# A decoder layer on one core: the same instructions, stepped through in another order on each of five engines

## The reference

```
x = x + attn(layernorm(x))            # stage a: 8 heads of 128, one shared key and value head, causal mask
x = x + xattn(layernorm(x), ctx, ...) # stage b: 16 heads of 16 over a context of 256,
                                      #   with a bias per batch, head, row and column, and a key mask
x = x + moe(layernorm(x))             # stage c: gate picks 2 of 8 experts, and one shared FFN;
                                      #   hidden = square(relu(x @ w1)), out = hidden @ w2
```

## Time and profile before

| | |
|---|---|
| median of 3 runs | 2403.15 us (2397.21 to 2403.51) |
| the profiled execution, its own time | 2400.63 us |
| its span | 2398.8 us |
| granted TensorE clock, mean over the span | 0.954 of full speed |
| busy: TensorE, VectorE, ScalarE, GpSimd | 2130.8, 1987.0, 2079.4, 1786.7 us |
| DMA traffic | 367.16 MB, 153 GB/s on average |

### The profile page before, as it was taken

One profiled execution on the slowest core, in us unless ns is written; L12 is line 12 of the kernel. 1 busy time (PEld: TensorE's weight loads), 2 busy tenths in 40 slices (PEclk: granted clock), 3 DMA queues, 4 the chain that ended last, 5 costly groups with the idle time before them and its releaser, 6 DMA issues.

```text
span 2398.8 us, 73036 instructions
## 1 busy us (share of the span) xinstructions
PE 2130.8 (89%) x24128; PEld 1855.2 (77%) x24128; DVE 1987.0 (83%) x6672; ACT 2079.4 (87%) x6065; POOL 1786.7 (74%) x1899
## 2 busy tenths in 40 slices
...
GB/s 148 113 173 155 168 146 162 171 153 160 159 155 142 173 157 158 162 155 138 169 155 164 161 157 163 145 174 160 161 163 156 150 147 158 162 160 157 142 145 22
DMA packets 711784, 367.16 MB, mean 153 GB/s; under 512 B 561392, under 2 KB 659952, under 8 KB 711408
## 3 DMA queue, kind: packets, MB, share of 16 engines
...
## 4 chain that ended last, share of the span: by engine, by line
PE 48%; DVE 21%; issue 14%; ACT 13%; POOL 2%; DMA 2%; SPq 0%; DVEq 0%; ACTq 0%; POOLq 0%
PE ps_a_misc L965 13%; PE ps_c_hidden L965 10%; PE ps_c_out L965 9%; PE ps_a_scores L1025 4%; DVE b_neg_scores L828 3%; DVE g_mask L898 2%; PE ps_b_misc L1102 2%; PE ps_b_scores L1088 2%; ACT ps_b_probs L664 2%; PE ps_a_misc L1044 2%; DVE b_probs_hi_lo L835 2%; ACT ps_b_probs L662 2%; ACT b_probs_hi_lo L672 2%; DVE g_weights L920 1%; DVE g_sum L913 1%
## 5 line engine op out<-in xcount | busy, mean ns | idle before, releaser
L520 POOL TENSOR_TENSOR bias<-bias,b_mask 128x512 f32<-128x512 f32 x512 | 646.4, 1274 | 7.2 <-DMA bias<-in_bias 7.0
L835 DVE TENSOR_TENSOR b_probs_hi_lo<-ps_b_probs,b_probs_hi_lo 128x512 f16<-128x512 f32 x512 | 351.8, 687 | 128.9 <-ACT b_probs_hi_lo L672 127.3
L828 DVE CUSTOM_DVE_ANT_0 b_neg_scores<-ps_b_scores,bias 128x256 f32<-128x256 f32 x1024 | 389.3, 417 | 72.0 <-PE ps_b_scores L1088 60.4
L534 POOL TENSOR_TENSOR c_hidden<-c_relu 128x512 f32<-128x512 f32 x288 | 299.8, 1041 | 152.7 <-ACT c_relu L690 138.0
L541 POOL TENSOR_TENSOR c_hidden_lo<-c_hidden,c_hidden_hi 128x512 f16<-128x512 f32 x288 | 334.2, 1160 | 59.8 <-issue 39.4
L662 ACT ACTIVATE ps_b_probs<-b_neg_scores,b_neg_max 128x256 f32<-128x256 f32 x512 | 245.4, 479 | 144.0 <-DVE b_probs_hi_lo L835 108.7
L965 PE MATMUL ps_c_hidden<-c_xT_hi,w_hi 128*128 128x256 f16 x1152 | 325.1, 282 | 40.1 <-ACT c_relu L690 40.0
L965 PE MATMUL ps_c_out<-w_hi,c_hidden_hi 128*128 128x256 f16 x1152 | 316.1, 274 | 29.0 <-DVE acc L936 28.9
L965 PE MATMUL ps_c_hidden<-c_xT_lo,w_hi 128*128 128x256 f16 x1152 | 324.0, 281 | 0.0
L965 PE MATMUL ps_c_hidden<-c_xT_hi,w_lo 128*128 128x256 f16 x1152 | 323.6, 281 | 0.0
L965 PE MATMUL ps_c_out<-w_hi,c_hidden_lo 128*128 128x256 f16 x1152 | 316.3, 275 | 0.0
...
## 6 DMA issues: line engine op xcount, KB each, us to landing
bias<-in_bias SPq DMA_DIRECT2D x256, 512.0 KB, 4.1
q_stack<-qk_scratch SPq DMA_DIRECT2D x256, 64.0 KB, 3.6
...
k_stack_even<-qk_scratch SPq DMA_DIRECT2D x128, 64.0 KB, 2.9
```

The lines of the kernel that those rows point to most:

```text
L520: gp.tensor_tensor(part, part, b_mask[:, :], ALU.add).then_inc(b_c_ok, 1)
L534: gp.tensor_tensor(c_h[:, :], c_r[:, e % 2, :], c_r[:, e % 2, :], ALU.mult).then_inc(c_sq_ok, 1)
L828: last = dve.tensor_tensor_reduce(out=b_t[:, u, c, :], in0=ps_bs[:, c * T:(c + 1) * T], in1=bias[:, slot, at:at + T], scale=-2.0, scalar=3 ...
L835: dve.tensor_tensor(b_p2[:, j % DEPTH, :, 1, :], ps_bp[:, :].rearrange("p (c t) -> p c t", c=CT), b_p2[:, j % DEPTH, :, 0, :], ALU.subtrac ...
```

## The change

The table ORDERS is replaced by another one. Each engine's list holds the same entries as before, 33 for SP, 47 for GpSimd, 111 for ScalarE, 120 for VectorE, 89 for TensorE; their order, their lags and the place where a list begins differ. No step's code is touched. The file grows by a line, so that each line of code behind the table has a number higher by one in the changed kernel. The diff, cut to the first and last rows of TensorE's list:

```
@@ -74,48 +74,49 @@
...
     tensor="""
-        a_s:5@3 c_f2:8@6 a_s:6@3 b_wo:0@5 a_pt:2@3 a_pv:1@3 a_s:7@3 b_s:0@4 b_s:1@4 a_pt:3@3 a_pv:2@3 c_T:0@5
...
-        c_f2:7@5 b_pv:13@4 b_pv:14@4 b_pv:15@4 a_s:4@2 a_pt:1@2 a_pv:0@2 b_o:0@4""",
+        b_pv:1@4 c_f2:1@5 c_f1:5@5 b_s:7@4 a_pt:6@3 b_pv:2@4 a_pv:5@3 c_f2:2@5 b_s:8@4 c_f1:6@5 a_pt:7@3
...
+        b_s:0@3 a_s:7@2 b_s:1@3 c_T:0@4 a_pt:4@2 b_s:2@3 c_gate:0@4 c_f1:0@4 b_s:3@3 a_pv:3@2 c_f1:1@4 b_s:4@3
+        c_f1:2@4 a_pt:5@2 c_f2:0@4 b_s:5@3 c_f1:3@4 a_pv:4@2 b_pv:0@3 b_s:6@3 c_f1:4@4""",
```

More of the change, by code:

```diff
@@ L76 @@
     sync="""
[L77 to L80, removed]
+        b_pT:8@5 b_pT:9@5 b_pT:10@5 b_load:5@5 b_pT:11@5 b_pT:12@5 b_split_q:0@4 a_T:0@3 b_pT:13@5 b_load:6@5
@@ L81 @@
+        b_store_q:0@4 b_load:7@5 b_pT:14@5 b_store_k:0@4 b_pT:15@5 b_stack_q:0@4 b_stack_k:0@4 b_load:0@4
+        c_f2:8@6 b_pT:0@4 b_mask:0@4 b_pT:1@4 b_load:1@4 a_ln:0@3 b_pT:2@4 b_pT:3@4 b_load:2@4 b_pT:4@4 b_pT:5@4
+        b_load:3@4 b_pT:6@4 b_pT:7@4 b_load:4@4""",
     gpsimd="""
-        b_comb:9@5 b_comb:10@5 b_comb:11@5 c_lo:4@6 c_f1:5@6 c_lo:5@6 c_f1:6@6 b_comb:12@5 a_ln:0@3 b_ln:0@4
-        b_comb:13@5 b_comb:14@5 a_kv:0@3 b_comb:15@5 c_lo:6@6 a_q:0@3 b_split_q:0@4 c_f1:7@6 c_lo:7@6
```

64 lines of the change are left out of this document (33 added, 31 removed).

## The result

The changed kernel takes **2438.43 us** (median of 4 runs, 2437.49 to 2439.81) against 2400.52 us for the kernel before (4 runs, 2397.21 to 2403.51): a ratio of 1.0159, 95% interval 1.0141 to 1.0177. It is slower by 38 us; the prediction said 10 us faster, with a range that ended at 2434. Lines of code have numbers higher by one.

A forecast was written before the change was run, and what follows sets the result against it. The prediction took no single engine as the bound, only holes between steps: 2400.6 - 13 (31 periods at 70.05 instead of 70.46 us) + 3.5 (filling) = 2391, stated as 2390 us, range 2352 to 2434.

The forecast's parts named there:

- The stall of q and k: TensorE's wait before b_s:0 for copies filling q_stack and k_stacks; predicted gone with its slow clock, 47 us less.
- The payback: New waits the change brings in each period: 0.5 to 2.5 us, taken at 1.1.
- Stage a later: a_kv and a_q:0 move behind b_s:15 on TensorE; claimed to cost nothing by itself.
- a_v_lo: VectorE's a_kv, ahead of b_s:15, waits for its input from TensorE: 0 to 1.4 us per period, taken at 0.3.
- c_f1:8 behind c_f2:4: ScalarE's relu waits for this later FFN product on TensorE: 0.5 to 1.1 us per period, taken at 0.8.
- GpSimd, priced at nothing: GpSimd's b_split_k ahead of a_kv and context split ahead of a_q:3; claimed free, otherwise a_s:6 late by one piece.
- Filling: Time before the first a_wo: last four weight pieces come after a_pv:7 of batch 0, +3.5 us (0 to +6).
- Draining: Stage c of the last batch keeps its order: 0, give or take 3 us.
- A reordering leaves every busy number as it is: All engines: claimed that reordering changes no busy time and can move only the holes between steps.
- Rival 2: End of stage a holds b_s:0 every period, TensorE waiting for VectorE (a_oT_lo), clock 0.95: 2430 us, chance 0.27.
- Rival 3: No change: the holes only move, held by stage a's chain or c_f1:8's relu: 2400 to 2404 us, chance 0.15.
- the rule beside it: Improve the most-contended engine; taken strictly, a change that takes nothing off any engine would leave 2400 us.

The follow-up runs named there:

- e9: Kernel before, order untouched, with six of the eight copies of the k stack left out (low-order products of stage b's scores missing): 2360.75 us, ratio 0.9838.
- e8: Kernel before with one part of the change alone, stage b's transpose and query projection ahead of stage a's: 2451.79 us, ratio 1.0199.
- e3: Changed kernel with a_kv on VectorE moved behind b_s:15 and b_p:14: 2462.97 us, ratio 1.0265.
- e7: Kernel before with c_f2:4 behind a_wo and c_f1:8 behind b_s:12 on TensorE, and matching moves on VectorE and ScalarE: 2422.83 us, ratio 1.0084.
- e6: Changed kernel with c_f1:8 put ahead of c_f2:4 on TensorE, directly behind a_wo: 2461.48 us, ratio 1.0248.
- e5: Changed kernel with b_pv:3, b_pv:5 and b_pv:6 on TensorE moved to where TensorE waits anyway: 2423.80 us, ratio 1.0095.
- e11: Changed kernel with ten entries on TensorE, ScalarE, VectorE and GpSimd moved by up to six places, off its chain or into holes: 2386.76 us, ratio 0.9944.
- e2: Kernel before with a_pt:2 and a_pv:1 on VectorE and a_pt:3 on TensorE put ahead of b_s:0: 2439.55 us, ratio 1.0154.

## Why the prediction was wrong

- **The stall of q and k** was taken as gone, worth 47 us. Right: it went (1 wait in place of 22), the clock is 1.00, and e9 measured 40 us for it. The 47 took every period at 68.95 us; their mean in e9 is 69.22. Had nothing else moved, the change would by this have come out near 2364 (2400.5 - 40 + 3.5, an estimate).
- **The payback**, taken as 1.1 us per period with bounds of 0.5 and 2.5, is the step that failed: 71.80 - 68.95 = 2.85, 31 x 1.75 = 54 us more than summed, above its own bound (the first period, 66.1 us, takes nearly 6 us off). Its terms:
  - "Stage a later ... by itself it costs nothing, because the work only changes sides" is the sentence that was wrong: what is put ahead of a step on the chain was priced at nothing. e8 prices b_T and b_q ahead of a_kv and a_q:0 at 51 us; a period of it without the stall takes 70.95 us, 2.0 more than before, and this is the largest share known. Work only changes sides if the chain runs through the engine that does it. Here it runs through a_kv and a_q:0 themselves, and what is put ahead of them lengthens it.
  - a_v_lo, 0.3 us (0 to 1.4): the wait is there and is 2.3 us per period (73.4 / 32). What it costs is not shown: e3 only moved it. By the rows of the chain, ScalarE is busy without a hole from b_q to a_q:0 while VectorE idles, so it is ScalarE's order that counts there.
  - c_f1:8 behind c_f2:4, 0.8 us: its predicted wait came alone in e7 (22 us, 0.9 per period) and not in the changed kernel (15.5 us against 27.7 before). TensorE does end c_f1:8 at 1229.20, 3.1 us behind a_wo's end at 1226.06, as summed (3.3); it is ScalarE that I had too early, at 2.2 us, where it is free only at 3.1. e6 shows that undoing it costs 23 us. The cause I named, the relu behind one more product, missed c_sq:6, which needs c_f2:4.
  - GpSimd, priced at nothing: VectorE's wait for the bias is 0.8 us per period (26.5 / 32), and a_s:6 does come late behind the context's split, the case that I named and set aside, by 0.48 us (13.8 us in 29 waits). No run tells what either is worth; in the period shown VectorE takes up a_s:6 at 1260.33, right behind its a_pv:1 (done at 1260.32).
  - The rest, 2.85 - 2.0 = 0.85 us, may lie in the three b_pv on the chain (14.6 us in e5, 0.5 per period) and the gate steps, 9.0 - 8.4 = 0.6 us longer by their place beside GpSimd's work. Together they are more than the rest, and neither was tried in the kernel before, so this last share is argued and not shown.
- **Filling** +3.5 us: 4.1, the last piece at 70.50 + 1.84 = 72.3 where I had near 71. **Draining** 0: -1.6.
- **"A reordering leaves every busy number as it is"** does not hold: VectorE, with the same instructions, is busy 1987.0 us before, 1974.9 in the changed kernel and 1923.1 in e11; the gate's small instructions beside GpSimd's work are a part of it.
- **The rivals.** Rival 2 had the sign and nearly the time (2430) but not the mechanism. One of its signs came: TensorE waits for a_oT_lo (33.1 us in 64 waits), 0.36 us of it ahead of a_pv:2; but that is far from 1.91 us and held up VectorE by some 0.2 us at most in the period shown, and the clock stayed at 1.00. That the time came near 2430 is luck. The mechanism is real in e2, where it turned a removed stall into 39 us of loss. Rival 3 did not hold, nor did the rule beside it, taken as strictly as there (the Trainium skill, Perfetto Trace Analysis, Identifying Performance Opportunities: improve the most-contended engine): e11 runs the same instructions on every engine as the change, and is 52 us faster.
